# The reciprocal factors of a normalization move to a PSUM bank, four multiplications become one, and one copy on ScalarE changes its place

## The reference

```
e = stack([tbl_f[ids[:, f]] for f in range(26)])               # gather
x = layer_norm(dense @ Wd.T, gd, bd)                           # 128 values of a sample
y = layer_norm(einsum('bnd,ed->bne', e, Ws), gs, bs)           # over the 128 of e, for each of 26 rows
y = einsum('bne,pn->bep', y, Wsi)                              # 26 rows mixed to 32
y = layer_norm(y, gsi, bsi)                                    # over the 32, for each (sample, e)
T = concat([x, y.swapaxes(1, 2)]);  Z = T @ T.T                # 33 x 33 products of a sample
z = layer_norm(Z[lower triangle] @ Wl.T, gl, bl) * mask        # 512, 384 of them kept
h = relu(relu([z, dense] @ W_top1 + b) @ W_top2 + b);  y = h @ W_top3
```

## Time and profile before

| what | us |
|---|---|
| median of 3 executions (621.01 to 622.87) | 621.14 |
| the profiled execution, its whole time | 624.07 |
| its span (first to last instruction) | 621.9 |
| gathers run on GpSimd | 3.1 to 536.1 |
| sixteen interactions on TensorE (L397) | 126.55 to 601.49 |
| GpSimd's indirect DMA instructions, busy | 402.7 |

### The profile page before, as it was taken

The page is one execution under the profiler, slowest core; times in us unless marked ns, Lnnn a source line. Parts: engine busy times, 40 slices in busy tenths (PEclk is TensorE's granted clock), DMA queues, the critical chain, the costliest instruction groups (busy, mean ns, idle before and its releaser), DMA issues.

```text
span 621.9 us, 17561 instructions
## 1 busy us (share of the span) xinstructions
PE 522.8 (84%) x6955; PEld 390.4 (63%) x6955; DVE 518.9 (83%) x1073; ACT 295.7 (48%) x730; POOL 403.4 (65%) x422
## 2 busy tenths in 40 slices
PE   1462777689999999999999999999899899988886
PEld 1352555547676767676767676676767577756566
DVE  3499689999999999999998989898989789996610
ACT  0410243545555546464645465555546364635422
POOL 6777775777777777777777777777777777400000
PEclk9955877899999999999999999999999899998999
DMA  7311111111111111111111121111111111100000
GB/s 181 104 25 33 27 29 30 27 35 27 35 29 35 28 37 28 36 27 27 38 27 36 27 38 28 35 29 37 27 38 28 27 27 27 20 1 2 1 1 2
DMA packets 22609, 20.22 MB, mean 33 GB/s; under 512 B 12016, under 2 KB 14720, under 8 KB 22528
## 3 DMA queue, kind: packets, MB, share of 16 engines
q0 software_dynamic: 13312, 13.66, 12.3%
q1 hardware_dynamic: 8400, 4.33, 2.7%
q10 hardware_dynamic: 816, 1.11, 0.6%
HBM read 19.07 MB, written 0.01 MB: 31 GB/s over the span
## 4 chain that ended last, share of the span: by engine, by line
PE 41%; DVE 21%; issue 15%; POOL 9%; ACT 8%; DMA 4%; SPq 2%; ACTq 0%; DVEq 0%; POOLq 0%
POOL emb L255 9%; PE b_y L342 7%; PE b_l L397 7%; PE b_l L414 6%; PE b_l L423 5%; PE b_z L354 4%; DVE nrm L774 3%; DVE V L807 3%; DMA emb<-in_tbl,idx 3%; PE b_mix L330 3%; ACT mixed L501 3%; PE b_a L312 2%; DVE yb L789 2%; DVE byn L784 2%; PE b_a L321 2%
## 5 line engine op out<-in xcount | busy, mean ns | idle before, releaser
L255 POOL DMA_INDIRECT emb<-in_tbl,idx x416 | 402.7, 968 | 132.8 <-issue 117.6
L506 ACT ACTIVATE sq<-yb 128x1024 f32<-128x1024 f32 x64 | 67.7, 1057 | 154.8 <-DVE yb L789 154.8
L789 DVE TENSOR_TENSOR yb<-b_y,bias_y 128x1024 f32<-128x1024 f32 x64 | 78.1, 1220 | 20.3 <-PE b_y L342 19.8
L342 PE MATMUL b_y<-mixed,projw 64*128 64x512 f32 x256 | 74.0, 655 | 24.2 <-ACT mixed L501 24.1
L807 DVE TENSOR_TENSOR V<-yb,rstd_y 128x256 f32<-128x256 f32 x256 | 91.9, 422 | 2.2
L796 DVE TENSOR_REDUCE var_y<-sq 128x32 f32<-128x1024 f32 x64 | 77.8, 1216 | 7.0 <-ACT sq L506 5.6
L397 PE MATMUL b_l<-wlt,zt 128*128 128x512 f32 x160 | 72.9, 602 | 0.8 <-issue 0.8
L330 PE MATMUL b_mix<-mix,byn 128*128 128x128 f32 x512 | 72.3, 287 | 0.0
L321 PE MATMUL b_a<-gram_w,embt 128*128 128x128 f32 x416 | 64.7, 298 | 6.0 <-ACT embt L490 5.2
L490 ACT ACTIVATE embt<-b_a 128x512 f32<-128x512 f32 (+1 forms) x64 | 33.0, 516 | 76.6 <-PE b_a L312 76.5
L354 PEld LDWEIGHTS b_z<-V 128*32 128x32 f32 x4096 | 46.0, 111 | 34.5 <-issue 17.8
(11 more groups left out here) (131 smaller groups left out, 686.8 us busy)
## 6 DMA issues: line engine op xcount, KB each, us to landing
emb<-in_tbl,idx POOLq DMA_INDIRECT x416, 2.5
dense<-in_r_dense_t SPq DMA_DIRECT2D x16, 128.0 KB, 2.2
V<-in_L_rec_Wl ACTq DMA_DIRECT2D x1, 1056.0 KB, 5.2
w<-in_W_top SPq DMA_DIRECT2D x2, 512.0 KB, 6.4
w<-in_W_top SPq DMA_DIRECT2D x1, 768.0 KB, 5.3
out_y<-y_sb SPq DMA_DIRECT2D x16, 0.5 KB
idx<-in_ids SPq DMA_DIRECT2D x1, 195.0 KB, 5.1
wd<-in_L_rec_Wd SPq DMA_DIRECT2D x1, 128.0 KB
```

Source lines behind the costliest of these rows:

```text
L255: pool.indirect_dma_start(out=emb[t % 2][:, f, :], out_offset=None, in_=tables[f], in_offset=bass.IndirectOffsetOnAxis(ap=idx[:, t, f:f + ...
L342: last = nc.tensor.matmul(b_y[:, j2, :], projw[r, :], mixed[c % 2][r, :], start=True, stop=True, tile_position=(64 * j2, 0))
L789: nc.vector.tensor_tensor(yb[c % 2][:, :, :, :].rearrange("e h s p -> e (h s) p"), b_y[:, :, :].rearrange("e h (s p) -> e (h s) p", p=NP), ...
```

## The change

`rstd_y` is no longer two SBUF tiles: it is one set of 32 columns in the bank `b_z`, right behind the gram matrices. The four multiplications of a quarter (8 of its 32 groups each) become one over all 32. As the bank is shared with TensorE and ScalarE, VectorE's reciprocal now also waits until ScalarE has copied the gram matrices of the quarter before (`zs_copied`), and ScalarE's copy of them is issued earlier in its quarter.

```diff
-        rstd_y = [sb(f"rstd_y{h}", [P, 32]) for h in range(2)]
...
+        rstd_y = b_z[:, 8 * GRAM:8 * GRAM + 32]
...
                 if ab:
                     copy_embt(*ab)
+                if (last := part(h, PROJECT + 2)):
+                    copy_zs(*last)
                 if (t := tile(h, LAYER1 + 1)) is not None:
                     relu1(t, 0)
                 if (last := part(h, PROJECT + 1)):
...
                 if (t := tile(h, INTERACT_NORM)) is not None:
                     scale_o(t)
-                if (last := part(h, PROJECT + 2)):
-                    copy_zs(*last)
...
                 after(dve, y_scaled, 4 * t + c - 1)
-                nc.vector.reciprocal(rstd_y[c % 2][:, :], std_y[c % 2][:, :]).then_inc(rstdy_done, 1)
+
+                after(dve, zs_copied, 4 * t + c)
+                nc.vector.reciprocal(rstd_y, std_y[c % 2][:, :]).then_inc(rstdy_done, 1)
                 dve.wait_ge(rstdy_done, 4 * t + c + 1)
                 after(dve, gram_done, 4 * (t - 2) + c + 1)
-                for j2 in range(2):
-                    for m in range(0, 4, 2):
-                        s = 16 * j2 + 4 * m
-                        last = nc.vector.tensor_tensor(V[t % 2][:, j2, c, m:m + 2, :, 0:NP].rearrange("e m q p -> e (m q) p"),
-                                                       yb[c % 2][:, j2, 4 * m:4 * m + 8, :],
-                                                       rstd_y[c % 2][:, s:s + 8].unsqueeze(2).broadcast_to([P, 8, NP]), ALU.mult)
-                last.then_inc(y_scaled, 1)
+                nc.vector.tensor_tensor(V[t % 2][:, :, c, :, :, 0:NP].rearrange("e h m q p -> e h (m q) p"), yb[c % 2][:, :, :, :],
+                                        rstd_y.rearrange("e (h s) -> e h s", h=2).unsqueeze(3).broadcast_to([P, 2, 16, NP]),
+                                        ALU.mult).then_inc(y_scaled, 1)
```

## The result

The changed kernel takes 628.46 us (median of 7, 627.96 to 629.81) against 621.37 for the kernel before in the same comparison (7 executions, 619.49 to 625.28). The ratio is 1.0099, 95% interval 1.0080 to 1.0117: slower by 1%. The profiled execution took 628.18 us, its span is 626.4 (before 621.9).

A forecast was written before the change was run, and what follows sets the result against it. Two loops within about 1% were taken as the bound: gathers, and TensorE with ScalarE. From the profiled 624.07, -1.3 +8.1 -2.2 +2.0 +0 +1.8 gave +8.4, 632.5; from the median, 631.7; stated 632, range 622 to 637.

The forecast's parts named there:

- One multiplication: VectorE's four multiplications as one at `yb`'s 1.22 us: 0.21 us a quarter gained, counting only before 126 us, -1.3 us.
- Factors in PSUM: GpSimd's gathers beside `V` lose their 6.8 us excess, floor about 32.45 a tile; worth something only if gathers stay slower.
- The copy's 0.43 us: ScalarE's `zs` ahead of `std_y` delays the projection: +0.06 or +0.43 in quarter I, +0.43 in II and III, hidden in IV.
- Behind the projection TensorE stands nowhere, so no slack takes these back: TensorE has no later waits to absorb the copy's delay, so a tile pays the full 0.92 us.
- the tile of 33.46: Steady tile not held by gathers: 32.54 + 0.92 = 33.46 us; ten such tiles give +8.1 us.
- The base of 32.54: Period of TensorE's loop with ScalarE, read from one tile not held by gathers, 223.22 - 190.68 = 32.54 us.
- The tile of 35.7 and two more: Tile with TensorE's 2.61 us gather wait loses that wait, -2.2 us; two further tiles, from the same 0.92, +2.0.
- The added wait: VectorE's reciprocal waiting for `zs_copied` costs nothing beyond the move, as `std_y` already stands behind that copy on ScalarE.
- The end: Last quarter I: the copy waits for the gram behind the 4.5 us interaction, delaying `std_y` and layer 2, +1.8 us.
- gathers stay the bound: Rival, faster: gather relief counts and the copy's delay is hidden, 613 or up to 619 us; chance 0.14.
- the multiplication is slow: Rival, slower still: VectorE's new multiplication takes 2.28 us (1.22 + 1.06), 643 us in all; chance 0.04.
- They cancel: Rival, 621 ± 1.9 us: unseen idle covers half of the 0.92 and the end costs nothing; chance 0.06.

The follow-up runs named there:

- copy first: Changed kernel with the copy of the gram matrices as ScalarE's first instruction of a quarter, ahead of `embt`: 619.98 us, ratio 0.9948.
- 23 gathers: Three of a tile's 26 features set once and not gathered: kernel before 615.79 us (ratio 0.9873), changed kernel 624.03 us (1.0023).

## Why the prediction was right

The sign and the mechanism were right, and 628.46 lies in the range; the size was over: +7.1 us in the medians (621.37 to 628.46), +6.2 by the ratio, where the forecast was about +11. By its own steps:

- *One multiplication*: 1222 ns, forecast 1.22, and no gain in the steady tiles. Ahead of the first interaction the profiles show -2.7 us where -1.3 was forecast, and that isn't shown to be the multiplication's: with four multiplications and only the copy moved this stretch ends at 124.50, 2.05 earlier than before, and it differs by 2.3 us between two executions in which its program is the same (126.53 and 124.23, copy first). The profiled kernel before also had a clock of 0.50 from 30 to 60 us, the changed one 1.00. The -1.3 stays untested.
- *Factors in PSUM*: the long gathers beside `V` are gone; with its factors in SBUF the one multiplication lengthened them even more. The Trainium skill (SBUF — State Buffer, Who interferes with whom) was cited for this, and the runs agree: 54 are lengthened beside the two-SBUF-input form, none in the changed kernel beside the PSUM form. That the relief is worth nothing behind a slower loop was shown by the move alone: 4.8 us of lengthened gathers, and the same steady tiles.
- *The copy's 0.43 us*: right in the waits (+0.42 and +0.41 in II and III, 0 in IV, quarter I 1.02 for 0.99) and in ScalarE's spacings. The copy made twice confirms it, with IV's cover used up.
- *The step that was mis-sized is "Behind the projection TensorE stands nowhere, so no slack takes these back"*, and with it the tile of 33.46. Forecast +0.92 on an undisturbed tile; measured +0.55 (32.15 to 32.70 with 23 gathers). TensorE did stand elsewhere: 0.38 us in front of `embt` in III, and in II it stood 0.12 for `z` (layer 2 at 297.25, behind a projection that ends at 297.13). A longer wait at the projection took those waits over. The base of 32.54 was too high as well: the undisturbed loop takes 32.15, and 32.54 was one tile with two grams of 1.02 and 1.01. That the changed tile came to 33.16, near the 33.46, is in part luck: 32.15 and 0.55 give 32.70, and the other 0.46 came with the gathers, in a term that the prediction didn't have (the grams, below). Ten tiles moved +4.8 instead of +8.1.
- *The tile of 35.7 and two more*: -2.6 and +1.9, forecast -2.2 and +2.0. The 35.7 was more than the wait of 2.61 us for a gather: the granted clock was 0.50 behind it, from 483.8 to 486.9 us.
- *The added wait*: no wait for `zs` shows in front of the changed kernel's reciprocal; where the copy comes later it is 101.3 us of VectorE's time.
- *The end*: +3.3, forecast +1.8. The copy's wait for the gram was foreseen (589.89 and 590.32, each 1.2 later than the forecast's 588.73 and 589.16, as this stretch began 1.2 later); these 1.8 came as forecast. Left out of the sum was the clock, which the prediction named only as a possibility: after TensorE's 3.25 us of waiting the granted clock was 0.50 (593.9 to 596.2), and layer 2 ran 3.14 us and not 2.02 (+1.1).
- *The rivals*: that gathers stay the bound, and that the multiplication is slow, are both excluded by the rows above. "They cancel" was right in its first half: waits that I didn't see covered 0.37 of the 0.92. Its second half, an end that costs nothing, was wrong. Between the first rival and the forecast it was decided by TensorE's undisturbed loop, 32.70, against GpSimd's floor of 32.45: a margin of 0.25 us a tile, not of the 1.0 that the prediction saw.

## What to carry to other kernels

When data moves to a bank that another engine reads, count the order that the sharing forces, and not only the access: here the order was the whole price. Read it at the engine that executes in order between two waits of the critical one, even if that engine is half idle, and look for a place where it waits already: in the kernel before, 0.43 us four times a tile cost 1.5% behind `embt` and 0.4% ahead of it. A delay at one wait counts only so far as the waits behind it don't shrink, so add up all waits of the critical engine in a period before charging it in full; and look at the last quarter apart, where what covered a copy is gone and where, in this run, the clock fell to 0.50 behind the longer wait.

## What the hardware did that I had not expected

A quarter's gram matrices are the same 64 small matmul records each time, yet at a granted clock of 1.00 they take 0.77 us or up to 1.04. In the changed kernel, GpSimd and TensorE:

```profile
400.21 0.94 POOL L257 DMA_INDIRECT emb<-in_tbl,idx  x1 [0.30 <-issue]
400.90 1.03 PE L356 MATMUL b_z<-V 128*32 128x34 f32 x64
401.46 0.94 POOL L257 DMA_INDIRECT emb<-in_tbl,idx  x1 [0.30 <-issue]
```

The next gather starts 0.56 us into the gram. Sorted by that distance, the grams between 160 and 530 us of all twelve traces (seven at a lower clock left out):

| next gather starts | cases | gram, us |
|---|---|---|
| 0.0, 0.1 | 24 | 0.99 to 1.01 |
| 0.2 | 43 | 0.77 |
| 0.3 | 41 | 0.78 to 0.88 |
| 0.4 | 53 | 0.86 to 0.98 |
| 0.5 | 91 | 0.95 to 1.03 |
| 0.6 | 53 | 0.77 to 1.04 |
| 0.7 to 0.9 | 95 | 0.77 |
| 1.0 to 1.2 | 32 | 0.77 to 0.96 |
| 1.5 and more | 98 | 0.77 to 0.79 |

In the mean the four grams of a tile take 3.11 us in the kernel before with 23 gathers and 3.50 with 26, and in the changed kernel 3.27 and 3.71; these 0.44 us are nearly all that lies between its tiles of 32.70 and 33.16. So gathers that nobody waits for go with about 0.4 us more a tile. It is a correlation; nothing was run that holds the gather's place fixed, and the cause is open.

An operand or a result in PSUM cost VectorE nothing that shows: 1222 ns beside 1226 from SBUF for the multiplication, and a mean of 340 ns for the reciprocal beside 332. The some 65 ns by which the Trainium skill (Perfetto Trace Analysis, Optimizing Scalar/DVE Operations) puts PSUM's access above SBUF's don't show here either.
